# A decoder layer's middle stage: in slots after a long attention unit, TensorE turns the first half of the scan's state ahead of the values product

## The reference

```python
# attention: 4 batches x 16 heads, 512 x 512 scores
scores = einsum("bqkgd,bskd->bkgqs", Qg, K) / scale     # causal mask, softmax
out = einsum("bkgqs,bskd->bqkgd", attn, V)
# scan: 4 batches, 512 channels, 16 states each
state = state * exp(d[..., None] * A) + (d * u)[..., None] * b[:, None, :]
y = einsum("bdn,bn->bd", state, c)
```

## Time and profile before

| | |
|---|---|
| median of 3 runs | 1220.5 us (1220.27 to 1222.01) |
| the profiled execution, its own time | 1220.22 us |
| its span, first to last instruction | 1218.5 us |
| TensorE matmul busy | 1074.8 us (88%) |
| VectorE busy | 809.6 us (66%) |
| ScalarE busy | 668.0 us (55%) |
| GpSimd busy | 673.1 us (55%) |
| mean granted TensorE clock | 0.98 of full |

### The profile page before, as it was taken

The page is one execution under the profiler, slowest core; times in us unless marked ns, Lnnn a source line. Parts: engine busy times, 40 slices in busy tenths (PEclk is TensorE's granted clock), DMA queues, the critical chain, the costliest instruction groups (busy, mean ns, idle before and its releaser), DMA issues. The chain is left out here.

```text
span 1218.5 us, 18629 instructions
## 1 busy us (share of the span) xinstructions
PE 1074.8 (88%) x6368; PEld 642.7 (53%) x6368; DVE 809.6 (66%) x1199; ACT 668.0 (55%) x1438; POOL 673.1 (55%) x587
## 2 busy tenths in 40 slices
PE   7999828888888888888888899999999989999993
PEld 3444416555555555555555544544444456666651
DVE  5477769999999999999999657741571023323327
ACT  3566668888888988888888722411111012222210
POOL 1033369999999999999999670201124025445420
PEclk9999959999999999999999999999999999999997
DMA  6210000110111011102222030202215433433229
GB/s 207 88 36 19 19 17 28 36 36 28 36 36 36 28 36 36 32 31 62 87 87 80 10 140 35 104 34 104 70 69 190 138 105 123 129 128 129 68 69 366
DMA packets 51932, 94.74 MB, mean 78 GB/s; under 512 B 9918, under 2 KB 18110, under 8 KB 51840
## 3 DMA queue, kind: packets, MB, share of 16 engines
q1 hardware_dynamic: 44320, 72.82, 18.2%
q0 software_dynamic: 7520, 20.72, 5.5%
HBM read 74.51 MB, written 20.84 MB: 78 GB/s over the span
## 5 line engine op out<-in xcount | busy, mean ns | idle before, releaser
L604 POOL TENSOR_TENSOR w_all<-w_all 128x512 f32<-128x512 f32 x256 | 320.8, 1273 | 1.6 <-DVE w_all L778 1.2
L778 DVE TENSOR_TENSOR_SCAN w_all<-da,w_all 128x512 f32<-128x512 f32 x256 | 298.0, 1206 | 0.0
L712 ACT ACTIVATE da<-w_all,a_flat 128x512 f32<-128x512 f32 x256 | 179.5, 701 | 9.0 <-PEq L96 7.7
L683 PE MATMUL yb<-ident,w_all 128*128 128x128 f32 x1024 | 162.6, 282 | 7.3 <-DVE acc L786 7.3
L633 PE MATMUL sc<-w_all,attn 32*128 32x384 f32 (+3 forms) x512 | 106.1, 491 | 44.3 <-ACT w_all L720 21.7
L720 ACT ACTIVATE w_all<-sc,neg_max 128x128 f32<-128x128 f32 (+3 forms) x256 | 134.1, 540 | 17.5 <-DVE neg_max L770 16.5
L659 PE MATMUL ob<-w_all,v 128*32 128x128 f32 x1280 | 94.9, 278 | 52.6 <-ACT w_all L729 52.6
L683 PEld LDWEIGHTS yb<-ident,w_all 128*128 128x128 f32 x1024 | 114.2, 142 | 36.9 <-issue 30.7
L770 DVE TENSOR_REDUCE neg_max<-sc 128x2 f32<-128x256 f32 (+3 forms) x128 | 104.3, 814 | 35.0 <-PE sc L636 35.0
L1195 POOL TENSOR_TENSOR w_all<-w_all 128x512 f32<-128x512 f32 x24 | 29.4, 1225 | 165.1 <-ACT w_all L1392 165.1
L729 ACT ACTIVATE w_all<-tb 128x256 f32<-128x256 f32 (+2 forms) x192 | 102.7, 535 | 29.8 <-PE tb L648 29.8
(11 more groups left out here) (198 smaller groups left out, 1670.9 us busy)
## 6 DMA issues: line engine op xcount, KB each, us to landing
w_all<-b_scratch SPq DMA_DIRECT2D x64, 256.0 KB, 3.3
w_all<-in_w_up SPq DMA_DIRECT2D x16, 512.0 KB, 5.4
w_all<-in_w_down SPq DMA_DIRECT2D x16, 512.0 KB, 6.7
w_all<-sorted_y SPq DMA_DIRECT2D x16, 512.0 KB, 11.4
attn<-in_x SPq DMA_DIRECT2D x4, 1024.0 KB, 7.0
w_all<-in_x SPq DMA_DIRECT2D x16, 256.0 KB, 4.1
norms<-attn SPq DMA_DIRECT2D x4, 1024.0 KB, 4.3
out_dram<-acc SPq DMA_DIRECT2D x16, 256.0 KB, 8.6
```

The lines of the kernel that those rows point to most:

```text
L604: pool.tensor_tensor(dbu[:, k, :], keep["du"][i // N][:, k * T:(k + 1) * T], b_all[i % 2][:, :], ALU.mult).then_inc(pool_dbu.sem, pool_dbu ...
L683: last = pe.transpose(yb[which][:, k * P:(k + 1) * P], state[i % 2][:, k, t * P:(t + 1) * P], ident[:, :])
L712: act.activation(da[unit % 2][:, :], keep["dt"][i // N][:, k * T:(k + 1) * T], ACT.Exp, scale=keep["a_flat"][:, unit % (N * KD):unit % (N ...
L778: dve.tensor_tensor_scan(state[i % 2][:, k, :], da[unit % 2][:, :], dbu[:, k, :], 0.0, ALU.mult, ALU.add).then_inc(dve_scan.sem, dve_scan. ...
```

## The change

In slots whose `weigh_v` belongs to a long unit ((g - 3) % 4 is 2 or 3), TensorE does `turn_state(g - 2, 0)` ahead of `weigh_v(g - 3)` and not behind it. In the other two of four slots the order stays. The count of instructions, their waits and the other queues stay as they are.

```diff
             scores(0)
             for g in range(UNITS + 3):
+                late = (g - 3) % NT >= 2
+                if 0 <= g - 2 < UNITS and late:
+                    turn_state(g - 2, 0)
                 if 0 <= g - 3 < UNITS:
                     weigh_v(g - 3)
                 if 0 <= g - 2 < UNITS:
-                    turn_state(g - 2, 0)
+                    if not late:
+                        turn_state(g - 2, 0)
                     if spread_in(g) is not None:
                         spread(spread_in(g))
                     else:
```

## The result

The changed kernel takes 1198.7 us (median of 4 runs, 1197.6 to 1200.0) against 1220.4 us before: a ratio of 0.9819, 95% interval 0.9807 to 0.9830, so 21.6 us or 1.8% less. The forecast was 1201 us, with a range of 1195 to 1210.

The account below looks back on a forecast made before the run. The prediction took a loop through several engines as the bound, with VectorE waiting for late TensorE. Terms 11.3 (slots 1, 2), 7.7 (slots 5, 6) and 0.4 (end) made 19.4 us saved, forecasting 1201 us, range 1195 to 1210.

Parts of the forecast that it names:

- The waits and whose they are: Middle stage of `mix`, per eight slots: VectorE waits 2.47 of 32.58 us, each time because TensorE is late.
- the signs that the prediction named: Profile after: group about 31.35 us, L659's wait about 0.3, `top(3)` and `top(7)` about 0.4, `top` in slots 2, 6 about 0.2.
- Slot 2, 0.74: Slot 2 of eight, with a spread: 0.74 us saved between `weigh_v` and `spread`, read from the stage's last slot.
- The 0.58 of the ordinary gap: Slot 2: the saving if an ordinary gap of 0.20 us stood between the two tiled groups.
- Slot 6, 0.38: Slot 6 of eight, no spread: 0.38 us saved by the state group leaving its place; the gap behind L659 stays.
- slot 5's 0.10: Slot 5 of eight: gains 0.10 us, since `weigh_v` stands 1.08 us behind `weigh_c`, against 0.99 in slot 1.
- Slots 1 and 5, 0.01 and 0.10: Moved transposes don't fit into the wait, as `dve_acc` comes late (0.11 us handover): gains only 0.01 and 0.10 us.
- B: Rival: the joint into `weigh_v` costs nothing, slots 1 and 5 gain 0.17 us more each: 1196 us; chance 0.11.
- C: Rival: joints are dearer, slots 1 and 5 lose 0.30 us each: 1210 us; chance 0.16 together with D.
- D: Rival: GpSimd or ScalarE takes over; 1210 us if GpSimd held back half; chance 0.16 together with C.
- E: Rival: slower; slots 1 and 5 put TensorE's queue behind `dve_acc`; 1226 us at 0.8 us a pair; chance 0.07.
- F: Rival: nothing moves, the freed time returns as another wait in front of the scores: 1220 us; chance 0.04.

Follow-up runs that it names:

- e3: Kernel before, with the new order only in slot 2 of each eight (the one with a spread): 1209.7 us, group of eight slots 31.84 us.
- e4: Kernel before, but in slot 2 `spread` directly behind `weigh_v` and both state halves behind it, no transposes moved ahead: 1216.6 us, group 32.29 us.
- e2: Kernel before, with the new order only in slots 1 and 5 of each eight: 1216.2 us, group 32.36 us.
- e11: Changed kernel, with both halves of the state's transposes ahead of `weigh_v` in slots 2 and 6: 1190.6 us, group 30.69 us.
- e6: Changed kernel, with two transposes done a second time in slots 1 and 5: 1205.4 us, group 31.64 us.
- e9: Changed kernel, with the new order in slots 3 and 7 too, so in all but slots 0 and 4: 1198.6 us, group 31.20 us.
- e8: Changed kernel, with the new order in all slots: 1235.4 us, groups of 31.40 to 35.72 us.

## Why the prediction held, step by step

**The waits and whose they are.** Right: VectorE's 2.47 us of waits in a group were all TensorE's lateness, and shortening TensorE's slots shortened the group by what they had to give (31.20 in the place of the 31.35 forecast). Of the signs that the prediction named, the waits of 0.46 and 0.43 before `top(3)` and `top(7)` came as said (about 0.4); the 0.13 left before `top` in slots 2 and 6 is less than the 0.2 said, and L659's listed wait of 0.49 is more than the 0.3.

**Slot 2, 0.74.** Measured 0.74 in e3, and taken from the one place where the new sequence already stood. The 0.58 of the ordinary gap would have been too low by 2.4 us. e4, in which the joints between the two tiled groups go and the transposes stay, gives 0.29, so that there is more to gain than the transposes is shown by itself. One step was not worked out: 0.74 was read on the way to the copy of `r_all`, and `top(3)`, which waits for scores, was given the same. The scores moved up by 0.72, so this held.

**Slot 6, 0.38, with slot 5's 0.10.** Mis-sized, too low. Between the starts of `top(6)` and `top(7)` it is 4.71 us in the earlier trace rows and 4.28 after (443.27 to 447.55): 0.43. The second half of the state starts 0.16 behind two transposes that stand behind a gap (445.36 to 445.52), where I had left the 0.22 of the old place (457.52 to 457.74).

**Slots 1 and 5, 0.01 and 0.10.** Right in kind, low in size: e2 gives 0.22 for both. The joint was 0.17 as assumed (423.83 to 424.41 is 0.58). The handover from VectorE was not: 423.05 + 0.72 to 423.83 is 0.06 and 438.92 + 0.73 to 439.70 is 0.05, where I took 0.11 from a place at which L659 stands ahead of the waiting transposes. Ahead of these stand plain transposes. That the kind of group ahead is the reason was not tested by itself.

**Rivals.** B (no joint) is out, by the 0.17 in the loads; C too, as the joint is no dearer. D: GpSimd had 22.4 us of waits left, and e11 shrinks the group to 30.69 us with GpSimd following. E did not come true in slots 1 and 5, but its loop is real: e6 shows that the 0.22 us added there is paid in full. F, the freed time turned into another wait in front of the scores, shows in slot 6 alone, and only from e11 on.

**The sum.** 19.4 us forecast, 22.7 in the span of the profiled execution, 21.6 in the medians. With the measured sizes the same sum is 15 x 1.38, 0.64 for the 16th pair without a spread (1.38 - 0.74) and 0.4, together 21.7. So the terms that were too low, slot 6 and slots 1 and 5, account for the 2.2 us between the forecast and the medians. In the span: 15 groups at 1.38 are 20.7; the end of the stage gives 0.4, as forecast; and 1.65 us come from the first group (31.37 us from the first `top` to the first reciprocal before, 29.72 after), of which slots 5 and 6, that 16th pair, explain 0.6. The rest is the clock at the stage's start, by stretch, before:

```profile
180.00:184.00 4.00, 3.82 (x15) 1.33 (x14) 3.12 (x4) 2.78 (x8) 3.42 (x4) 0.50 0.20 66
184.00:188.00 4.00, 4.00 (x28) 3.25 (x27) 3.98 (x6) 3.51 (x8) 2.35 (x3) 0.64 0.00 0
```

and after:

```profile
180.00:184.00 4.00, 3.81 (x25) 2.35 (x25) 4.00 (x5) 3.26 (x9) 3.44 (x4) 0.87 0.24 66
184.00:188.00 4.00, 2.69 (x28) 1.99 (x27) 4.00 (x5) 4.00 (x11) 3.28 (x4) 1.00 0.00 0
```

It rose to 1.00 at about 187 us before and at 181 after, some 6 us earlier. This is not the change: e3 and e4 have the order of before in the first group, and theirs took 31.28 us with the late rise and 30.32 with the early one; and e9, whose later groups are as long as the changed kernel's, took 30.70 with a late one. So 1 us of an execution's time hangs on it, and single spans can't be compared closer than that.

**The rule weighed.** The Trainium skill, TensorEngine Tiling, Key Properties, has a drain at each change of tiling mode. The measurements agree: 0.20 behind L659 ahead of plain transposes, none ahead of L670, and e4, which only takes changes of mode out of slot 2, is 0.29 us a group shorter.

## What to carry to other kernels

Two waits of the same length for the same releaser can be worth 0.6 us and 0.1 us: ask when the work that is to fill them could start, and test it with two more instructions in each place. Before an independent group is moved in front of a wait, look for the same sequence anywhere in the trace, and take the time from there. And reorder no more than is worth something: letting two short waits of TensorE stand close together, with little work between, cost the clock in most groups, and with it more than the whole gain.

## What the hardware showed that I had not expected

- TensorE's granted clock fell from 1.00 to 0.50 (2.4 to 1.2 GHz) behind 3.1 us in which it was busy for 1.32 us, with the longest single wait at 0.99 us. It stayed there some 7 us, under full load. The same stretch with the same waits was once not followed by a fall (404.10 to 407.20). In the changed kernel the same wait of 1.00 us with `weigh_v` behind it does nothing to the clock. e8 came out 37 us slower than the changed kernel, nearly all of it by the clock. The Trainium skill, TensorE: Matmul & The Clock Gate, section "HAM oscillation — how this bites in real kernels", describes a clock that falls each time round a loop; there the waits were for DMA and several microseconds long. In e8 the longest wait of the matmuls in that stretch was the 0.99 us above.
- Two tiled groups of the same shape go through without a joint, and their loads mix across the boundary (the row of L659 shows 12 of its 16, the last 4 come among those of L670): both took 1.87 us of loads to the next plain group, in e4 and in the changed kernel alike. Before, with the transposes between them, it was 1.00 us from L659 to the next plain group and 1.01 from L670 (440.96 to 441.97).
